# Two attentions and a feed-forward: v transfers by parity, root chains on GpSimd, new engine orders, a pipelined attention, an earlier set-up

## The reference, cut to what matters

```python
# first branch, once
qkv = x_normalised @ W_qkv;  q, k = layernorm(q), layernorm(k)
attn = softmax(causal(q / sqrt(8) @ k.T));  out = (attn @ v) @ W_out
# second branch, six times
q, k = l2norm(q) * q_scale, l2norm(k) * k_scale      # per head of 64
q, k = rotate(q, cos, sin), rotate(k, cos, sin)
x = x + (softmax(8 * q @ k_window.T + mask) @ v_window) @ Wo
a, g = split(layernorm(x) @ W1 + b1);  x = x + (a * gelu(g)) @ W2 + b2
```

## Time and profile before

| | us |
|---|---|
| median of 3 runs | 4520.82 |
| lowest, highest | 4502.21, 4533.23 |
| the profiled execution | 4523.09 |
| its span, first to last instruction | 4521.3 |
| windowed layers, within it | 863 to 4509 |
| attention, from the first maxima to the projection | 146 to 844 |

### The profile page before, as it was taken

The page is one execution under the profiler, slowest core; times in us unless marked ns, Lnnn a source line. Parts: engine busy times, 40 slices in busy tenths (PEclk is TensorE's granted clock), DMA queues, the critical chain, the costliest instruction groups (busy, mean ns, idle before and its releaser), DMA issues. The chain is left out here.

```text
span 4521.3 us, 174754 instructions
## 1 busy us (share of the span) xinstructions
PE 4000.7 (88%) x67089; PEld 2684.5 (59%) x67328; DVE 3651.6 (81%) x7085; ACT 2863.2 (63%) x5681; POOL 2582.5 (57%) x2483
## 2 busy tenths in 40 slices
PE   4588888689999999999999999999999999999997
PEld 2234434266666666666666666666666666666665
DVE  7666656388888888888888888888888888888886
ACT  4255555466666666666666666666666666666664
POOL 5111111366666666666666666666666666666663
PEclk7699889899999999999999999999999999999998
DMA  2322220222222322222222222222232222222221
GB/s 79 53 29 25 33 28 6 72 55 58 58 56 56 80 56 58 56 56 78 58 57 56 56 60 75 56 56 56 56 80 56 56 56 56 65 56 56 56 56 48
DMA packets 176299, 250.32 MB, mean 55 GB/s; under 512 B 46918, under 2 KB 65988, under 8 KB 175300
## 3 DMA queue, kind: packets, MB, share of 16 engines
q1 hardware_dynamic: 176196, 248.94, 22.7%
HBM read 39.08 MB, written 8.39 MB: 10 GB/s over the span
## 5 line engine op out<-in xcount | busy, mean ns | idle before, releaser
L958 PE MATMUL w_px<-w_wqkv,w_xs 128*128 (+1 forms) x2304 | 1164.0, 607 | 61.4 <-DVE w_kr L1450 31.8
L1342 POOL TENSOR_TENSOR w_qr<-w_raw,w_tc 128x512 f32<-128x512 f32 x384 | 485.6, 1276 | 512.7 <-ACT w_raw L1172 333.5
L1349 POOL TENSOR_TENSOR w_qrot<-w_raw,w_tc 128x512 f32<-128x512 f32 x384 | 481.6, 1277 | 454.0 <-ACT w_raw L1172 454.0
L958 PEld LDWEIGHTS w_px<-w_wqkv,w_xs 128*128 128x128 f32 x2304 | 380.7, 192 | 266.5 <-issue 185.3
L593 DVE TENSOR_REDUCE a_row_max<-a_ring 128x1 f32<-128x640 f32 (+6 forms) x352 | 352.0, 1028 | 176.0 <-PE a_ring L422 171.0
L1356 POOL TENSOR_TENSOR w_qr<-w_qr,w_qrot 128x512 f32<-128x512 f32 x384 | 489.2, 1274 | 0.0
L1364 POOL TENSOR_TENSOR w_qr<-w_qr,w_rn 128x512 f32<-128x512 f32 x384 | 401.8, 1046 | 143.2 <-DVE w_rn L1472 135.7
L524 ACT ACTIVATE a_probs<-a_wide 128x512 f32<-128x512 f32 (+1 forms) x608 | 324.3, 573 | 249.5 <-remote 153.9
L1372 POOL TENSOR_TENSOR w_kr<-w_kr,w_rn 128x512 f32<-128x512 f32 x384 | 397.0, 1044 | 65.6 <-DVE w_rn L1472 65.6
L563 POOL TENSOR_SCALAR_AFFINE_SELECT a_probs<-a_probs 128x512 f32<-128x512 f32 x128 | 81.5, 636 | 580.8 <-ACT a_probs L524 580.8
L1051 PEld LDWEIGHTS w_pw<-w_ot,w_wo 128*128 128x128 f32 x3072 | 367.8, 193 | 59.6 <-issue 49.5
(11 more groups left out here) (151 smaller groups left out, 9266.5 us busy)
## 6 DMA issues: line engine op xcount, KB each, us to landing
w_vw<-w_v SPq DMA_DIRECT2D x1152, 128.0 KB, 2.3
w_vw<-w_v SPq DMA_DIRECT2D x768, 64.0 KB, 2.0
a_q_stack<-q_parts SPq DMA_DIRECT2D x144, 64.0 KB
a_k_stack<-k_parts SPq DMA_DIRECT2D x144, 64.0 KB
w_wqkv<-in_L_ffn_Wqkv SPq DMA_DIRECT2D x6, 1536.0 KB, 6.0
q_parts<-ap_parts SPq DMA_DIRECT2D x8, 384.0 KB, 2.5
k_parts<-ap_parts SPq DMA_DIRECT2D x8, 384.0 KB, 2.5
w_wo<-in_L_ffn_Wo SPq DMA_DIRECT2D x24, 128.0 KB, 2.7
```

Of the source, the lines that this page charges most:

```text
L958: nc.tensor.matmul(px[bank_of(PX_USES, what, i, u)][:], xs[u][:], rhs, start=True, stop=True).then_inc(done, 1)
L1342: nc.gpsimd.tensor_tensor(by_head(qr[i][:]), by_head(raw[i][:]), wide(table(u, Q_COS)), ALU.mult).then_inc(q_straight[i], 1)
L1349: nc.gpsimd.tensor_tensor(halves(qrot[i][:]), swapped(raw[i][:]), split_table(u, Q_SIN), ALU.mult).then_inc(q_rotated[i], 1)
```

## The change

1. v is projected with its columns in the order of the heads' parity, so that each half of v holds one parity. The five transfers of a parity wait for their half of v alone and have their own semaphores, `v_windows[parity][u]`; TensorE waits for them in a step of its own before the values.
2. The clamp becomes a ScalarE instruction (`over` = Relu(ss - 1e-24), and the logarithm adds 1e-24 again). The Newton step of the factors goes to GpSimd as five instructions on 32 columns, and that of the layer norm as five on 2 columns.
3. The four bodies are rotated and reordered, and PX_USES and PT_USES with them.
4. In attention, the end of a step is made within the next step.
5. In set-up, the weights of attention are loaded in `prepare`; the stack loads of the first batch are issued between the stores of the turns; the stacks are zeroed as f32, and GpSimd, not VectorE, writes the rows of ones.

```diff
-WINDOW_DMAS = 10
+WINDOW_DMAS = 5
...
+            sp.dma_start(t.a_wqkv[:], t.awqkv_d).then_inc(t.a_loaded, 16)      # in prepare, and four more
...
+                    if n == FIRST_BACK:                                          # 5, in the loop of the stores
+                        sp.wait_ge(filled, 1)
+                        for m in range(SLOTS):
+                            sp.wait_ge(stored[m], 16)
+                    if n >= FIRST_BACK:
+                        for hg in range(GROUPS):
+                            for a in range(3):
+                                for j in range(3):
+                                    if FIRST_BACK + (9 * hg + 3 * a + j) * (N_TURNS - FIRST_BACK) // (9 * GROUPS) == n:
+                                        load_stack(sp, 0, hg, a, j)              # one transfer of q, one of k
...
-                for n in range(GROUPS):
-                    nc.vector.memset(k_stack[n][96:99, :, :], 1.0)
...
-                for buf in (*k_stack, *v_pad, *q_stack, neg_max):
-                    last = nc.gpsimd.memset(buf[:], 0.0)
-                last.then_inc(filled, 1)
+                for stack in (*k_stack, *q_stack):
+                    nc.gpsimd.memset(stack[:].bitcast(F32), 0.0)
...
+                for stack in k_stack:
+                    last = nc.gpsimd.memset(stack[96:P].bitcast(F32), TWO_ONES)
+                last.then_inc(filled, 1)
...
                 for kind, n in order:                                            # attention, TensorE, step(b, hg)
                     if kind == 0:
-                        maxima(b, hg, n)
-                    elif not is_first(b, hg):
+                        if n == 2:
+                            if has_ctx:
+                                values(GROUPS * b + (hg - 2), (hg - 2) % GROUPS, KC - 1)
+                            if has_scores:
+                                turn_maxima(b, hg)
+                        if n == 6 and has_ctx:
+                            turn_context(b, hg)
+                        if n == 10 and has_batch:
+                            turn_tokens(b, hg)
+                        if n == 14 and has_batch:
+                            project(b, hg)
+                        if has_max:
+                            maxima(b, hg, n)
+                    elif has_scores:
                         scores(n2, before, n)
...
-                turn_maxima(b, hg)
-                if not is_first(b, hg):
-                    values(n2, before, KC - 1)
-                    turn_context(n2, b, hg, TURN_CTX)
-                    if hg == 0:
-                        project(b, hg, PROJECT, 2 * GROUPS * b + 2)
...
-                if n == 0:                                                       # in maxima
+                if n == 3 and parts_of(alike(b, hg))[1]:
                     wait(pe, placed_act, 2 * GROUPS * b + 2 * hg)
...
+                if what == "v":
+                    rhs = wqkv[:, bass.ds(slot, 1), 2 * INNER:3 * INNER].rearrange("p s (n x d) -> p (s n) x d", n=4, x=4)[:, :, 2 * i:2 * i + 2]
...
+            def clamp(r, u):                                                     # ScalarE
+                ...
+                for i in range(2):
+                    chunk(act, k_summed[i], r, u)
+                    chunk(act, q_summed[i], r, u)
+                chunk(act, factors_ready, r, u, back=1)
+                nc.scalar.activation(over[:], ss[:], ACT.Relu, bias=less_tiny[:]).then_inc(clamped, 1)
...
+            def refine(r, u):                                                    # GpSimd
+                ...
+                pool.sem_clear(chain)
+                chunk(pool, seeded, r, u)
+                nc.gpsimd.tensor_tensor(ssc[:], over[:], tiny[:], ALU.add).then_inc(chain, 1)
+                nc.gpsimd.tensor_tensor(step[:], seed[:], seed[:], ALU.mult).then_inc(chain, 1)
+                pool.wait_ge(chain, 2)
+                nc.gpsimd.tensor_tensor(step[:], step[:], ssc[:], ALU.mult).then_inc(chain, 1)
+                pool.wait_ge(chain, 3)
+                nc.gpsimd.tensor_tensor(step[:], three[:], step[:], ALU.subtract).then_inc(chain, 1)
+                pool.wait_ge(chain, 4)
+                nc.gpsimd.tensor_tensor(rn[u][:], step[:], seed[:], ALU.mult).then_inc(factors_ready, 1)
+
+            def refine_x(r):                                                     # the same five on mv, eps, ls, lt, top
+                ...
+                nc.gpsimd.tensor_tensor(lr[:], lt[:], ls[:], ALU.mult).then_inc(f_chain, 1)
...
             def normalise_x(r):                                                  # VectorE: only this is left
-                wait(dve, f_seeded, r + 1)
-                ...
+                wait(dve, f_chain, r + 1)
                 for c in range(2):
                     ins = nc.vector.tensor_scalar(xnt[:, c, :], pf[:, c * P:(c + 1) * P], mv[:, c, 0:1], lr[:, c:c + 1],
```

More of the change, by code:

```diff
@@ L167, in attention, with load_stack @@
         neg_max = sb("neg_max", [P, S // P, AG, BAND], BF16)
+        stacked = [sem(f"stacked{n}") for n in range(GROUPS)]
+        FIRST_BACK = 5
+        TWO_ONES = struct.unpack("<f", struct.pack("<I", 0x3F803F80))[0]
+        def load_stack(engine, b, hg, a, j):
+            toks = bass.ds(b * S, S)
+            rows = slice(AG * AHD * hg, AG * AHD * (hg + 1))
+            at = AHD * (3 * a + j)
+            for stack, src in ((q_stack, t.q_parts_d[a]), (k_stack, t.k_parts_d[j])):
+                engine.dma_start(stack[hg][at:at + AHD, :, :], src[rows, toks].rearrange("(h r) t -> r h t", h=AG)
+                                 ).then_inc(stacked[hg], 16)
         with ExitStack() as pre:
@@ L317, in attention @@
         out_bank = ctx.enter_context(nc.psum_tensor("a_out", [P, S], F32))
-        stacked = [sem(f"stacked{n}") for n in range(GROUPS)]
         r_full, r_done = sem("r_full"), sem("r_done")
@@ L367, in over_batches @@
                     step(b, hg)
-            last()
+            for hg in range(2):
+                step(B, hg)
+        SCORES_FROM = 0.14
         def spread(costs, first):
@@ L402, in _ @@
                     sp.wait_ge(wide_full, NS * GROUPS * b + (NS * (hg + 1 - GROUPS)))
-                    stacks(b, hg)
+                    for a in range(3):
+                        for j in range(3):
+                            load_stack(sp, b, hg, a, j)
             for hg in range(GROUPS):
@@ L495, in step @@
                             values(n2, before, kc - 1)
-                turn_maxima(b, hg)
-                if not is_first(b, hg):
-                    values(n2, before, KC - 1)
-                    turn_context(n2, b, hg, TURN_CTX)
-                    if hg == 0:
-                        project(b, hg, PROJECT, 2 * GROUPS * b + 2)
-            def last():
-                n2, before = GROUPS * B - 1, GROUPS - 1
-                for w in range(NS):
-                    scores(n2, before, w)
-                    kc = score_units[w][0]
-                    if kc >= 1 and w == last_of[kc]:
-                        values(n2, before, kc - 1)
-                values(n2, before, KC - 1)
-                turn_context(n2, B, 0, 0)
-                project(B, 0, 1, 2 * GROUPS * B)
-            over_batches(pe, step, last)
+            over_batches(pe, step)
         @block.scalar
@@ L679, in windowed @@
         ident_bf = sb("ident_bf", [P, P], BF16)
-        eps = sb("eps", [P, 1])
+        tiny = sb("tiny", [P, 2 * HEADS])
+        less_tiny = sb("less_tiny", [P, 1])
+        three = sb("three", [P, 2 * HEADS])
+        eps = sb("eps", [P, 2])
+        near = sb("near", [P, 1])
+        top = sb("top", [P, 2])
         keep = sb("keep", [P, PAIRS_B])
@@ L733, in windowed @@
         q_straight, q_rotated, q_added, q_normal = two("q_straight"), two("q_rotated"), two("q_added"), two("q_normal")
[L734 removed]
+        v_projected, v_copied = two("v_projected"), two("v_copied")
+        v_windows = [two(f"v_windows{i}") for i in range(2)]
         tables_ready, clamped, logged, seeded, chain, factors_ready = (sem("tables_ready"), sem("clamped"), sem("logged"),
@@ L775, in _ @@
                 nc.vector.memset(eps[:], 1e-5)
+                nc.vector.memset(tiny[:], 1e-24)
+                nc.vector.memset(less_tiny[:], -1e-24)
+                nc.vector.memset(three[:], 3.0)
+                nc.vector.memset(near[:], math.log(NEWTON_AT))
+                nc.vector.memset(top[:], 1.5 / NEWTON_AT)
                 nc.vector.memset(keep[:, 0:1], 0.0)
@@ L940, in _ @@
             layer_loads(LAYERS - 1, False)
-            for u in range(2):
-                sp.wait_ge(v_windows[u], WINDOW_DMAS * 16 * steps)
+            for par in range(2):
+                for u in range(2):
+                    sp.wait_ge(v_windows[par][u], WINDOW_DMAS * 16 * steps)
         @block.tensor
@@ L1421, in sum_k @@
                 chunk(dve, k_squared[i], r, u)
+                chunk(dve, clamped, r, u, back=1)
```

(1 more changed line is left out.)

402 lines of the change are left out of this document (209 added, 193 removed).

## The result

The changed kernel takes 4147.9 us at the median of four runs (4144.9 to 4152.2) against 4518.1 us for the kernel before on the same chip (4502.2 to 4533.2): 0.918 of the time, 95% interval 0.915 to 0.922. The profiled execution has a span of 4150.4 us, 370.9 less than before.

| | before | after | gain |
|---|---|---|---|
| start to first maxima | 146.0 | 129.2 | 17 |
| first maxima to first windowed projection | 717.2 | 667.5 | 50 |
| windowed layers, to the finish | 3647.5 | 3343.1 | 304 |

A forecast was written before the change was run, and what follows sets the result against it. TensorE, 92% busy in the windowed layers, was taken to be held by its work, a wait before the second turning and the lower clock. 4523 - 289 - 98 - 2 = 4134 us, stated as 4135; range 4060 to 4370.

The forecast's parts named there:

- The windowed loop: Windowed layers: the wait before the second turning shrinks and the lower clock goes; period 37.58 to 34.6 us, gain 289 us.
- the chain after the first turning: Windowed loop, statistics through root to scaled x: durations and six hand-overs add to 4.6 us, up to 1 us more.
- the cover: Windowed loop: TensorE's work between first and second turning, falling by 0.9 to 5.6 us in the new order.
- the first and third rivals: GpSimd's short operations in the loop: first, GpSimd becomes the bound, 4309 us, chance 0.17; third, slower, 4803 us, chance 0.07.
- the line through the earlier trace: GpSimd's short operations, estimated from its 512- and 256-column times: 260 ns at 32 columns, 195 at 2.
- that is no term, since it was not the bound: Windowed loop: VectorE losing clamps, refinements and root, the root alone 2.6 of its 32.3 us, was credited no gain.
- The second rival: Wait before the second turning only changes its name, seed late or GpSimd within an add; 4363 us, chance 0.12.
- The attention term: Attention stage: a step's end moves behind the next step's first maxima; step 41.7 to 35.2 us, gain 98 us.
- residual wait: Attention step: the fourth maxima wait for ScalarE's placing; taken as 1.3 us, half of the context's 2.65 us wait.
- The set-up term: Set-up: early loads, memsets on GpSimd, interleaved stack loads; first maxima at 144 us, bounds 132 and 156, gain 2 us.
- so 72 x 64 KB take 68 us: Set-up: the stack loads at their lone 69 GB/s take 68 us, or 37 if stores fill the engines' idle share.
- The v split: Windowed loop: splitting v's transfers by parity was costed at nothing, being covered between copying v and the values.

The follow-up runs named there:

- both_on_vector: The changed kernel with the layer-norm root and the factors' clamp and refinement back on VectorE, new orders kept; 4283.8 us, ratio 0.948 to the kernel before.
- moves_in_old_orders: The kernel before with layer-norm root and factors' refinement on GpSimd and the clamp on ScalarE, all in the old orders; 4387.1 us, ratio 0.971.
- attention_old: The changed kernel with the preparation and whole attention stage of the kernel before, the windowed stage staying new; 4220.3 us, ratio 0.934 to the kernel before.
- the siblings: Follow-up variants of the changed kernel with its attention stage's instructions left the same; 37.7 or 37.8 us an attention step against 38.5.
- fill_3_6: The changed kernel with 3 idle 512-column matmuls before each turning of the maxima and 6 before each attention step's fourth maxima; 4129.8 us, ratio 0.913.
- stacks_late: The changed kernel with the first 36 stack loads issued after all stores, as before; 4137.5 us, ratio 0.915 to the kernel before.

## Why the prediction was right, point by point

Predicted 4135, measured 4148, with the range and the sign as forecast. Its terms: 289, 98 and 2 us; measured in the traces 304, 50 and 17. The three misses, 15 us too little, 48 too much and 15 too little, partly cancel, so that the total is only 13 us off is in part luck.

**The windowed loop** was right in its sum, and its mechanism is real: the wait goes, and the low clock with it. But it is not the only one at work. The period is 34.31 for 34.6; the chain after the first turning took 4.4 us for 4.6, the cover 5.9 for 5.6; the clock is 1.00 from 2000 to 3000 us; no xnt wait remains. GpSimd's unmeasured short operations, on which the first and third rivals hung, take what the line through the earlier trace rows gave:

```profile
L1469 POOL TENSOR_TENSOR w_step<-w_step,w_ssc 128x32 f32<-128x32 f32 x58 | 14.6, 252 | 4.6
L1488 POOL TENSOR_TENSOR w_lr<-w_lt,w_ls 128x2 f32<-128x2 f32 x30 | 5.9, 195 | 2.4
```

252 ns for 260 and 195 for 195; start to start a link is 0.27 us, so the root 1.17 us for 1.34. The Trainium skill ("GPSIMD Engine Reference", "Engine selection") puts GpSimd at about twice VectorE's time; here it is 252 against VectorE's unblocked 192 ns at 32 columns, 1.3 times. And VectorE's operations on 2 columns, which run 0.16 us alone, still had means up to 0.90 us when they came back beside GpSimd, in both_on_vector (L1609, above). That long one has a single tensor input, and the short L1611 two. The Trainium skill ("SBUF — State Buffer", "Who interferes with whom") names copies and tensor_scalar, too, as able to contend with GpSimd. The 0.90 us of this tensor_scalar against its shortest, 0.17, agrees; which of the four is hit changes with the order.

What the prediction did not see is that the remedy was there twice. It took the root's move as what closes the gap, and counted the new orders as costing 0.9 us of cover. They do cost some, 6.5 to 5.9, but they also take 1.5 us from the chain, with the root still on VectorE. The forecast chain of 4.6 us added up durations; it never compared them with the 8.0 us of the kernel before, in which the aggregation came 2.45 us after the turning. The runs: root alone in the old orders 210 us, orders alone about 160, both about 234 (35.05 against 37.51 us a period). The root's share with the orders there is 74 us with the factors on VectorE and 16 to 20 without. Each removes most of the same wait, and with it the same low clock, so the gains do not add. And "that is no term, since it was not the bound", of the clamps and refinements, failed: they are worth 62 to 120 us in the new orders and cost 80 in the old ones. The root's move by itself leaves a period of 35.25 us, not the 34.6 that was reckoned from it; the rest came from what was priced at nothing or as a cost. That the sum fits is luck to this extent. The second rival (GpSimd within another operation when the seed comes) is what moves_in_old_orders does.

**The attention term was mis-sized**, 50 for 98; attention_old gives 55 (72 less the set-up's 17), and with the clock of the siblings it would be some 61 (an estimate, 0.7 us more in each of 15 steps). The step forecast 31.95 us of work, 2.0 of idle time and 1.3 of residual wait. Measured, the work is 502.4 / 577 of 38.5, 33.5 us, and 5.0 are idle. With the waits filled the work is 511.3 / 551 of 36.8, 34.15; nine fillings at an estimated 0.22 (in fill_3_6 a matmul of 128 columns starts 0.22 us behind one of 512) take 2.0 of it, which leaves 32.2, about the forecast: so by this estimate 1.3 us of the miss is the clock, which the forecast took to be half recovered and which falls at each boundary; 1.7 us are idle time. The residual wait was named rightly, the fourth maxima behind ScalarE's placing (16.6 us in 15 waits, 1.1 each), but the turning's wait for the reductions (7.4 us) and the small ones behind each use of the two banks were folded into 6%.

**The set-up term was mis-sized**, 17 for 2: first maxima at 129.2 for 144, below the lower bound of 132. The step that failed is the time of loads and stores together, 61 us from 83 on, made of "so 72 x 64 KB take 68 us" and the stores. The loads began at 82.1 as forecast, but from 80 to 128 us the DMA engines moved 193 GB/s at a share of 0.66, and loads and stores were through together some 47 us after the first load. And behind the stores, as in stacks_late, the 68 us are not on the path at all: the first maxima wait for the first group's 18 loads only, 20 us. What the gain is made of in both forms is the memset tail, which stood in the earlier trace rows, and the earlier start.

**The v split**, costed at nothing, is worth nothing.

## What to carry to other kernels

Two edits that shorten the same chain earn its wait only once: measure each part on top of nothing and on top of the rest before crediting it. The root here was worth 210, 74 or 16 us, by what else was in the kernel. Add up a chain for the kernel before as well, and see whether it gives the length that the trace shows. A move between engines moves its place in a queue with it: the same refinement earned 62 us in one GpSimd and VectorE order and cost 80 in another. Before pricing a transfer, read which count the first reader waits for, and look for plain work between the last store and the first load.

## What the runs showed that was not expected

Matmuls without a reader, nine a step, raised the clock of the attention stage to 0.99, from 0.92 in the changed kernel and 0.95 in its siblings, and took 1.0 us from each step against the siblings. Identical attention stages had a clock of 0.92 in one kernel and 0.95 to 0.96 in six others (158 to 720 us), and 10 us between them. And a store of 384 KB took 6.2 to 6.4 us to land (medians) with stack loads in its queue, 2.5 us without. It delayed the stores, whose last was issued 17 us later, but not the first maxima, since by then the loads were done too.
